# Linear attention joined to the block of the layers: o-products on two banks, rotation tables in its steps 5 to 8, local attention begun at its step 32

## The reference, cut to what matters

```python
# 1. gated linear attention, 2 heads of 64 (x is normalized and modulated before it)
q = silu(x @ Wq); v = x @ Wv; log_f = log_sigmoid(x @ Wk + delta); k = -expm1(log_f)
S = S * exp(g_t)[..., None] + k_t[..., None] * v_t[..., None, :]; o_t = q_t @ S      # over t
o = rms_norm_by_head(o * sigmoid(x @ G1 @ G2)) * norm_w; x = x + gate * (o @ Wo)
# 2. two layers on y = modulate(layernorm(x)):
#    local attention (8 heads of 64, windows of 64, rotary tables with scales), then a gated MLP
q = l2norm(q) * q_scale; k = l2norm(k) * k_scale; q, k = rotary_xpos(q, k)
y = y + local_attention(q, k, v) @ wo
y = y + (a * gelu(g)) @ w2 + b2                  # a, g = layernorm(shifted y) @ w1 + b1
# 3. a convolution-like attention   4. sixteen experts
```

## Time and profile before

| | us |
|---|---|
| median of 3 runs | 1184.93 (1182.98 to 1184.94) |
| profiled execution, its own time | 1182.32 |
| its span, first to last instruction | 1180.5 |
| PE busy | 1060.1 (90%) |
| DVE busy | 899.6 (76%) |
| ACT busy | 850.7 (72%) |
| POOL busy | 660.2 (56%) |

### The profile page before, as it was taken

One profiled execution on the slowest core, in us unless ns is written; L12 is line 12 of the kernel. 1 busy time (PEld: TensorE's weight loads), 2 busy tenths in 40 slices (PEclk: granted clock), 3 DMA queues, 4 the chain that ended last, 5 costly groups with the idle time before them and its releaser, 6 DMA issues. The chain is left out here.

```text
span 1180.5 us, 33825 instructions
## 1 busy us (share of the span) xinstructions
PE 1060.1 (90%) x11683; PEld 729.0 (62%) x11683; DVE 899.6 (76%) x2972; ACT 850.7 (72%) x2674; POOL 660.2 (56%) x1070
## 2 busy tenths in 40 slices
PE   6689996599999999789799999998899799999996
PEld 4466674267777776556477777776566488853442
DVE  4799998478888888565588888887475655289998
ACT  2678884488988898423589888987345766478886
POOL 1578985688888888200588888887133400002222
PEclk9899998799999999899899999999799999999999
DMA  7000000021321211131112222122000343200000
GB/s 237 3 2 10 11 3 1 16 49 38 71 54 47 50 45 47 39 120 34 40 38 47 47 47 47 38 47 47 21 1 20 85 112 86 49 6 17 17 19 18
DMA packets 66498, 50.86 MB, mean 43 GB/s; under 512 B 42262, under 2 KB 53442, under 8 KB 66050
## 3 DMA queue, kind: packets, MB, share of 16 engines
q1 hardware_dynamic: 66339, 48.84, 16.3%
HBM read 21.41 MB, written 2.38 MB: 20 GB/s over the span
## 5 line engine op out<-in xcount | busy, mean ns | idle before, releaser
L1168 PE MATMUL psum<-wa_wqkv,wa_hT 128*128 128x512 f32 x384 | 190.9, 606 | 4.4 <-DVE wa_tmp L1032 3.2
L1124 ACT ACTIVATE wa_p<-psum,wa_nb 128x128 f32<-128x128 f32 x512 | 184.2, 399 | 4.3 <-DVE wa_nb L1048 4.2
L1048 DVE CUSTOM_DVE_ANT_0 psum<-psum,wa_bias 128x128 f32<-128x128 f32 x512 | 133.0, 323 | 51.4 <-PE psum L1197 51.4
L1014 POOL TENSOR_TENSOR wa_p<-wa_p,wa_rrs 128x512 f32<-128x512 f32 x128 | 133.3, 1041 | 49.1 <-DVE wa_rrs L1057 49.1
L1709 POOL TENSOR_TENSOR ex_total<-ex_total,mod 128x128 f32<-128x128 f32 x32 | 15.5, 485 | 211.3 <-DVE ex_total L1837 211.3
L1124 ACT ACTIVATION_READ_ACCUMULATOR wa_p<-psum,wa_nb 128x1 f32 x512 | 122.7, 240 | 0.0
L1884 ACT ACTIVATE cv_z_ex_yw<-psum,ex_w 128x128 f32<-128x128 f32 x384 | 107.0, 401 | 20.1 <-DVE ex_w L1813 7.7
L1955 PE MATMUL psum<-ex_wc,ex_hT 128*128 128x512 f32 x256 | 117.9, 603 | 3.4 <-DVE cv_z_ex_yw L1820 2.1
L985 POOL TENSOR_TENSOR wa_qr<-wa_qr,wa_tmp 128x512 f32<-128x512 f32 x64 | 81.9, 1280 | 64.3 <-DVE wa_tmp L1032 64.3
L1134 ACT ACTIVATE wa_pT<-psum 128x512 f32<-128x512 f32 x128 | 76.6, 598 | 40.2 <-PE psum L1177 40.2
L1177 PE MATMUL psum<-ident,wa_p 128*128 128x128 f32 x512 | 81.4, 283 | 10.1 <-ACT wa_kT L1117 3.2
(11 more groups left out here) (258 smaller groups left out, 3007.2 us busy)
## 6 DMA issues: line engine op xcount, KB each, us to landing
wa_vm<-wa_v SPq DMA_DIRECT2D x127, 128.0 KB, 2.3
cv_toep<-cv_zpad SPq DMA_DIRECT2D x32, 136.0 KB, 2.7
cv_toep<-cv_zpad SPq DMA_DIRECT2D x16, 264.0 KB, 4.2
wa_tabs<-in_rotations_dram SPq DMA_DIRECT2D x2, 2048.0 KB, 8.0
wa_rows<-y_rows SPq DMA_DIRECT2D x31, 128.0 KB
wa_rows<-y_rows SPq DMA_DIRECT2D x31, 127.0 KB
x_rows<-in_L_attn_x_dram SPq DMA_DIRECT2D x4, 512.0 KB, 5.8
out_dram<-x_rows SPq DMA_DIRECT2D x32, 64.0 KB, 1.5
```

Source lines behind the costliest of these rows:

```text
L1014: nc.gpsimd.tensor_tensor(p, p, cols_bc(rrs[:, t % 2, r, :], P), ALU.mult)\
L1048: m = nc.vector.tensor_tensor_reduce(out=s, in0=s, in1=edges, scale=-1.0, scalar=MAX_FLOAT, op0=ALU.add, op1=ALU.min, accum_out=nb[:, t % ...
L1124: e = nc.scalar.activation(pr[:, t % 2, r, h, :], sim_bank[r][:, P * h:P * h + P], ACT.Exp, bias=nb[:, t % 2, r, h:h + 1], scale=-1.0, acc ...
L1168: nc.tensor.matmul(bank, hT[:, t % 3, :], wqkv[:, INNER * k:INNER * k + INNER], start=True, stop=True).then_inc(done.sem, 1)
```

## The change

1. `linear_attention` no longer has a block; it returns a `Phase` per engine, and its phase stands first in the timetable of the layers. `AttentionInputs.first_loads`, `stage` and so on are called as before; the first rows staged by attention's own SP list now wait for the y rows they need.
2. On ACT `values` moves from the head of a step with lag 2 to its end with lag 1, and on POOL all lags are one higher: within linear attention each engine's order stays the same, save at the few steps with additions between.
3. The tables are made one at a time before DVE's steps 5, 6, 7 and 8.
4. `o_project` of tile 29 and 31 writes to bank 6 (`out`), that of 30 to bank 7. Tile 29 waits for `gated` of tile 31, tiles 30 and 31 wait for the `residual` two tiles back.
5. Steps 0 to 7 of the first local attention come after the linear steps 32, 34, 36, 40, 41, 42, 43 and 44.
6. Attention and MLP take other banks (a plain renumbering 0, 1, 2, 3, 5, 6 to 2, 3, 5, 0, 6, 1, the same in both layers). Buffers of the layers now lie over those of linear attention, ordered so that the last needed are the last overwritten.
7. The ACT table load at the beginning of the first attention is gone; `wa_kT` is cleared before attention step 2, and of `ml_mT` only the last third, before attention step 10.

```diff
 class Phase:
-    def __init__(self, stages, first, n, between=None, begin=None):
+    def __init__(self, stages, first, n, between=None, begin=None, longer=None, more=0):
...
-def linear_attention(c, y, load_next, prepare_next):
+def linear_attention(c, y, given, ctx):
...
+    TWO_BANKS = TILES - 3
+    o_product = lambda t: out if t >= TWO_BANKS and (t - TWO_BANKS) % 2 == 0 else wide
...
-                unrolled([(keys, 0), (modulate, 13), (distances, 0)], 0, between={16: lambda: prepare_next.gpsimd(gp)})
+        return Phase([(keys, 1), (modulate, 14), (distances, 1)], 0, TILES, begin=begin,
+                     between={16: lambda: given.gpsimd(gp)})
...
-                between[36] = lambda: prepare_next.vector(dve)
+        for k in range(4):
+            between[5 + k] = lambda k=k: given.vector(dve, k)
...
-                unrolled([(values, 2), (decays, 3), (normalize, 0), (inverse_rms, 6), (exps, 1), (y_normalize, 14),
-                          (logs, 1), (h_columns, 0), (squares, 5), (sigmoids, 1), (end_keys, 2), (y_scale, 10)], 0,
+        return Phase([(decays, 3), (normalize, 0), (inverse_rms, 6), (exps, 1), (y_normalize, 14), (logs, 1),
+                      (h_columns, 0), (squares, 5), (sigmoids, 1), (end_keys, 2), (y_scale, 10), (values, 1)], 0, TILES,
...
-                    take("wide", v_res[1], t)
-                    nc.tensor.matmul(wide[:, 0:GH * E], ogT[:, t % 6, :],
+            if t == TWO_BANKS:
+                v_og.wait(pe, TILES - 1)
+            else:
+                v_res[1].wait(pe, t - 1 if t < TWO_BANKS else t - 2)
+            nc.tensor.matmul(o_product(t)[:, 0:GH * E], ogT[:, t % 6, :],
...
-    def vector(self, dve):
+    def vector(self, dve, k):
         self.wait_layer(dve, 0)
-        for k in range(4):
-            self.scale_table(dve, k)
+        self.scale_table(dve, k)
...
-    BANKS = ((0, 1, 2, 3, 4, 5, 6, 7), (0, 1, 2, 6, 7, 5, 4, 3))
+    BANKS = ((2, 3, 5, 0, 4, 6, 1, 7), (2, 3, 5, 1, 7, 6, 4, 0))
...
-                         begin=lambda: nc.scalar.preload_act_table_set("natural_log_exp_and_others"))
+                         begin=(lambda: nc.scalar.preload_act_table_set("natural_log_exp_and_others")) if l else None)
...
-        nc.gpsimd.memset(mT[...], 1.0)
+        nc.gpsimd.memset(mT[:, :, LAST, :], 1.0)
...
+    LINEAR, ATT, MLP = TILES + 14, TILES + 5, GROUPS + 4
+    MERGED = {32: 0, 34: 1, 36: 2, 40: 3, 41: 4, 42: 5, 43: 6, 44: 7}
...
+    for s in range(LINEAR):
+        timetable.append((0, s))
+        if s in MERGED:
+            timetable.append((1, MERGED[s]))
```

More of the change, by code:

```diff
@@ L175, in step @@
         for f, lag in self.stages:
-            if 0 <= s - lag < self.n:
+            if 0 <= s - lag < self.n + (self.more if f is self.longer else 0):
                 f(self.first + s - lag)
@@ L201, in linear_attention @@
     MAX_STEP, MAX_SIG_LOG = 20.0, 41.0
-    with ExitStack() as ctx:
-        sb = c.sb(ctx)
+    with ExitStack() as own:
+        sb = c.sb(own)
+        ring = lambda name, n, *shape: sb("la_" + name, [P, n, *shape])
+        eps, heads = sb("la_eps", [P, 1]), sb("la_heads", [P, GH])
+        yst, ymv = ring("yst", 2, 6), sb("la_ymv", [P, TILES, 2])
+        lyv, ys, yb = (sb("la_" + n, [P, TILES]) for n in ("lyv", "ys", "yb"))
+        lms, rr = ring("lms", 2, GROUP * GH), ring("rr", 2, GROUP * GH)
+        ogT, sq = ring("ogT", 6, P), ring("sq", 3, P)
+        wog = sb("la_wog", [P, B, GH, E])
+        qe, attn = ring("qe", 3, Q_SLOTS, P), ring("attn", 3, GH, P)
+        sg, vk = ring("sg", 4, 2, P), ring("vk", 4, 2, P)
+        state = [sb(f"la_state{b}", [P, P]) for b in range(B)]
+        masks = sb("la_masks", [P, NLEV, P], U32)
+        keep = sb("la_keep", [P, P])
+        dist, dec = ring("dist", 2, 1 + SLOTS * P), ring("dec", 2, SLOTS, P)
         cT, ex4, sig4, silu = (sb(n, [P, 4]) for n in ("cT", "c_exp", "c_sigmoid", "c_silu"))
@@ L226, in linear_attention @@
[L226 to L269, removed]
@@ new lines, in linear_attention, with in_turn @@
+    sem = lambda name: c.sem(ctx, "la_" + name)
+    signal = lambda name, every=1: Signal(sem(name), every=every)
+    def in_turn(name, n, every=1):
+        s = sem(name)
+        return [Signal(s, k, n, every) for k in range(n)]
+    c_in, w_in = sem("c_in"), sem("w_in")
+    x_in = [sem(f"x_in{k}") for k in range(TILES // CHUNK)]
+    g_set, v_set, a_set, p_set = sem("g_set"), sem("v_set"), sem("a_set"), sem("p_set")
+    v_xst, v_xb = in_turn("v_xst_xb", 2, CHUNK)
+    a_lx, a_xs = in_turn("a_log_xs", 2, CHUNK)
@@ L842, in first_loads, with stage_normalized @@
         self.load_layer(sp, 0)
+        self.y_done = y_done
         for i, n in self.PORTIONS[:self.AHEAD]:
-            y_done.wait(sp, i + n - 1)
-            self.stage(sp, "attention", 0, i, n)
+            self.stage_normalized(sp, i, n)
+    def stage_normalized(self, sp, i, n):
+        self.y_done.wait(sp, i + n - 1)
+        self.stage(sp, "attention", 0, i, n)
     def gpsimd(self, gp):
@@ L964, in sync @@
                 if not l and portion and 1 <= portion[0] <= len(PORTIONS) - AHEAD:
-                    given.stage(sp, "attention", l, *PORTIONS[portion[0] + AHEAD - 1])
+                    given.stage_normalized(sp, *PORTIONS[portion[0] + AHEAD - 1])
                 if i == 8:
@@ L1018, in gpsimd @@
             return Phase([(scale_q, 2), (scale_k, 2), (scale_p(0), 3), (add_q, 1), (clip, 1),
-                          (scale_p(1), 3), (add_k, 1)], first, TILES, begin=None if l else lambda: at_start(gp))
+                          (scale_p(1), 3), (add_k, 1)], first, TILES,
+                         between=None if l else {s: lambda f=f: f(gp) for s, f in between.items()})
         def vector(dve):
```

898 lines of the change are left out of this document (458 added, 440 removed).

## The result

| | before | after |
|---|---|---|
| median, us (20 runs each, side by side) | 1184.72 (1178.82 to 1190.11) | 1176.97 (1173.46 to 1185.00) |
| ratio of the runs | | 0.9934, 95% interval 0.9920 to 0.9948 |
| span of the profiled execution, us | 1180.5 | 1172.2 |
| PE busy | 1060.1 (90%) | 1062.9 (91%) |
| DVE busy | 899.6 (76%) | 897.0 (77%) |

Faster by 0.66%, 7.8 us. The forecast of 1176.5 us was met to half a microsecond. The profile shows that this is luck in good part: the seam gained 3.6 us less than forecast, the tables cost 2.3 us less, what was forecast behind the seam cost less too, and the errors cancel.

What follows compares the result with a forecast made beforehand. Seam bound by waits and list order, attention behind it by PE, linear attention mostly by DVE. -11.9 + 0.8 + 0.3 + 3.3 = -7.5 us gave 1174.8; median placed 1.7 above, 1176.5 us, range 1173 to 1180.

Steps and rivals of the forecast that it cites:

- The sum: Whole kernel: seam -11.9, POOL's modulation 0.8, memset 0.3 and tables 3.3 give -7.5 us, 1174.8 us; median placed at 1176.5.
- Tables: Linear steps 5 to 8: each table lengthens its step by 0.8 us to 5.4, 3.3 us in all, bounds 2.0 to 5.1.
- Seam: From linear attention to the layers: first attention scores start 11.9 us earlier, at 216.6 us; bounds 9.8 to 14.4.
- The delay by ACT: Linear step 33: attention step 0 holds ACT at h_columns, so the decays of tile 30 start 1.5 us late.
- the clock term: Seam: low clock between linear step 35 and attention step 3 only, costing 1.5 plus 1.0 us, 2.5 in all.
- The queue behind step 1: Seam: linear step 35, with base_level and PE's last output, queues behind attention step 1; 6.6 and 3.1 us in series.
- Behind the scores: After the first scores: POOL's modulation in linear steps 41 to 45 costs 0.8 us, the mT memset 0.3.
- The signs named: Changed profile: scores near 220 us, table steps 5.4, residuals 1.3, decays 1.5 late, clock low only before scores, constant shift.
- Rival 1: Seam: no real overlap, inserted steps only stand in line; 9.8 us won there, total -5.4, 1178.5 to 1180 us; chance 0.17.
- Rival 2: Seam and tables: full overlap at 2.4 GHz, -14.4 + 2.0 = -12.4 us, 1170 to 1172 us; chance 0.12.
- Rival 3: Merged stretch: small pieces keep PE's clock low through attention steps 3 to 5, some 6 us a step, 1187 us; chance 0.04.
- Rival 4: Linear attention: regular steps take 0.2 us longer in all 30, eating 6 us; within 2 us of before; chance 0.05.

Runs made afterwards that it cites:

- 5: The changed kernel with every output product in bank 7 instead of two banks; ratio to the kernel before 0.9962, scores 40.8 us from tile 29.
- 9: The changed kernel with attention step 0 kept behind linear step 32, steps 1 to 7 moved behind 36 and 40 to 45; ratio to before 0.9894, scores 38.3 us from tile 29.
- experiment 4: The changed kernel with attention step 0 moved from linear step 32 to 34, right ahead of step 1; ratio to before 0.9894, scores 35.9 us from tile 29.
- 6: The changed kernel with attention steps 0 and 1 both behind linear step 35; ratio to before 0.9917, scores 33.8 us from tile 29.
- 1: The kernel before with only the rotation tables moved to DVE's linear steps 5 to 8; ratio to before 0.9949, tile 20 at 223.7 us from tile 29.
- 2: The kernel before with only the last output products on two banks; ratio to before 0.9973, scores 47.3 us from tile 29.
- 3: The changed kernel with no attention step among the linear ones; block, tables and banks stay; ratio to before 0.9878, scores 37.3 us from tile 29.
- 10: The changed kernel with attention steps 0 to 7 behind linear steps 36, 38 and 40 to 45; ratio to before 0.9877, scores 32.6 us from tile 29.
- 7: The changed kernel with attention steps 0 to 5 behind linear steps 36 and 40 to 44; ratio to before 0.9874, scores 34.3 us from tile 29.

## Why the prediction was right, step by step

**The sum.** Forecast -11.9 + 0.8 + 0.3 + 3.3 = -7.5 us. Measured at attention's tile 0: -8.3 for the seam, 1.0 for the tables, 0 for POOL and the memset: -7.3 (its residual at 246.39 against 253.66). At the end of the span it is 8.3, and 7.8 between the medians. The sum is right by luck, since none of its terms is: the seam brought 3.6 us less, the tables cost 2.3 us less, and of the 1.1 us for POOL and the memset nothing had come by tile 0 and 0.3 later on. The step from the profiled execution to the median has its share too: I placed the median 1.7 us above the sum, and it lies 3.0 above the profiled execution, 1176.97 to 1173.95, while the sum of 1174.8 was 0.9 too high.

**Tables, mis-sized: 3.3 us, measured 1.0.** I took 5.4 us for the length of a step; it was 4.96 to 5.00. (Four times 0.8 is 3.2; the 3.3 is a slip of 0.1.) The starts of DVE's instructions tell why. From `base_level` to clip it took 63.80 - 63.11 = 0.69 us before and 60.52 - 60.19 = 0.33 after: that is the wait for PE's projection, marked as 0.24. From `scaled` to the running sum 1.31 became 1.19, the wait for the log. These two I had, as 0.24 and 0.10. But the distances to `query` (1.28 to 1.13), to `keep_levels` (0.35 to 0.20) and to `base_level` (0.46 to 0.33) shrank as well, by waits too short to be marked in a row. Together 0.91 us, so that a table whose successor starts 1.19 us after it lengthens the step by 0.28. Over all: from `scaled` to `scaled` the four steps were 4.31, 4.55, 4.68 and 4.68 us and are 4.97, 5.00, 4.96 and 5.00, in sum 1.7 us more, and the next two won 0.7 back. 1.0 is under my lower bound of 2.0. That bound let a table of 1.28 us fill all the time in which DVE is not busy, 0.79 us, but 0.91 us were there to fill and the table takes up only 1.19 of a step. And "so it is not won back" was wrong by those 0.7 us. That I added nothing for the contention with POOL was right: POOL is busy 4.52 us of a step with a table, 3.51 before, and no row of DVE there waits for it.

**Seam, mis-sized: 11.9 us, measured 8.3.** By its own terms, after, from DVE's step 33 at 184.09:

| part | forecast at full clock | measured |
|---|---|---|
| attention step 0, linear steps 33 and 34 | 1.5 + 7.45 = 8.95 | 11.23 (to 195.32) |
| attention step 1 | 6.6 | 8.15 (to 203.47) |
| linear steps 35 and 36 | 3.1 + 1.3 = 4.4 | 5.09 (to 208.56) |
| attention step 2 | 5.9 | 7.57 (to 216.13) |
| steps 37 to 40, to the scores | 5.2 | 5.13 (to 221.26) |
| sum | 31.05 + 2.5 for the clock = 33.55 | 37.17 |

The delay by ACT was sized right: `scaled` comes 186.49 - 184.09 = 2.40 us into the step and came 0.95 us into it before, 1.45 more for the 1.5. The residuals too: 216.65 to 217.92 is 1.27 us, for 1.3. What failed is the place and size of the clock term, 2.5 us. I had it fall "between linear step 35 and attention step 3 only". It fell at 188.7 us already, at the end of linear step 33, where I had called the steps "as before", so that linear step 34 and much of what follows ran at 1.2 GHz as well, and the whole is 6.1 us over the terms at full clock instead of 2.5 (how much of the 6.1 is the clock's was not taken apart). That it is attention step 0's place that brings this is shown by its removal: in the three kernels that have step 0 behind linear step 32 (after, 5 and 9) the clock falls within linear steps 33 and 34, in the nine that have not it stays at 1.00 there, each by one profile. Moving it is worth 4.4 us (experiment 4), three times the 1.5 us of the wait. That PE's idle time of 1.2 us before the scores of step 33 is what drops the clock fits the rows but was not tried by itself.

**The queue behind step 1, in the sum but not seen as a choice.** The prediction has linear step 35, "and so PE's last output", queued behind attention step 1, and adds the two in series. That is how it runs, and another place is cheaper: 2.1 us from 4 to 6 (35.9 and 33.8), 2.0 us from the change to 9 (40.3 and 38.3), though in 6 step 0 moves too, and in 9 all later steps. That the 2.0 us are PE's wait for `base_level` alone is not shown.

**Behind the scores, mis-sized: 1.1 us forecast, 0.3 measured.** From the first scores to tile 0's residual it is 25.13 us after and 25.17 before; both hold one step at a low clock, and in 1, 2, 3, 9 and 10, which have none, it is 23.7 to 23.8. The change could have won these 1.4 us as well. POOL's y rows stand right before `scale_q`, in its timeline after,

```profile
220.49 0.46 POOL L326 TENSOR_TENSOR y_rows<-y_rows,mod 128x128 f32<-128x128 f32 x1
221.02 0.45 POOL L328 TENSOR_TENSOR y_rows<-y_rows,mod 128x128 f32<-128x128 f32 x1
221.43 1.04 POOL L1017 TENSOR_TENSOR wa_qr<-wa_qr,wa_rn 128x512 f32<-128x512 f32 x1
```

and cost little: PE's steps there are 7.95, 8.01, 7.88 and 8.01 us, against 7.89 before. From tile 0 to tile 8 the residuals are 0.3 us further apart than before, in two steps of 8.02 and 8.01 us and one of 7.95, the only one that experiment 3 has too. The step after the first scores is 9.18 us, over the 8.5 that I had named as a sign of error; in the row 221.26:230.44 the clock is at 0.73, and before a step of the same stretch took 9.29 us.

**The signs named.** Held: scores near 220 (221.26), single table rows, residuals at 1.3, decays 1.5 us late, steps of linear attention from 10 on equal within 0.05 us. Did not hold: table steps of 5.4 us, the clock's place, the constant shift. The shift is 7.0 to 7.3 us through the first layer's attention, then between 6.0 and 11.9 us, 8.3 at the end; the later seams differ by as much among kernels that are alike there.

**The rivals.** Rival 1, that each inserted step only stands in line, is the nearest account of the seam: with no step inserted at all (experiment 3) it is 3.0 us shorter at the scores than with three. Its figure of -9.8 for the seam is 1.5 us from the measured -8.3, mine 3.6. Its total of 5.4 us came out too small because it shared my terms for the tables and POOL. What it lacked is that inserting can cost more than nothing. Rival 2 (full overlap, -14.4) is what experiments 6, 7 and 10 reach in size, with 14.8, 14.3 and 16.0 us, by placing the steps behind the recurrence; its full clock they have not, since in all three the clock is at 1.2 GHz for a while before the scores. Rival 3, the clock kept low by pieces, was right in kind and too large: the clock is at 1.2 GHz in three spells, from 188.7, 202.4 and 219.4 us, each of them over in 7 to 10 us. The Trainium skill, TensorE: Matmul & The Clock Gate, HAM oscillation, warned of this; in this trace the clock does go down, up and down again, 0.71, 0.50, 0.80, 0.73, 1.00 by stretch, and the change is faster all the same. Rival 4 did not happen.

## What to carry to other kernels

Where two chains are laid into one in-order list, ask at each insertion what of the old chain is queued right behind it and who waits for that: here the first scores come 5.7 us later with attention's first step inside the recurrence (9) than with it behind (10; its second step stands elsewhere too). An insertion's price is its wait and what comes with it, here a fall of the clock; together they were three times the wait alone. Measure each part of a change by itself: here the tables' move alone came within 0.4 us of the whole to tile 20, and one part, the interleaving, took 3.0 us away. And when filler work is put into a step that is bound by a loop of short waits, expect it to fill waits too short to be marked: read the distances between the starts of the instructions, and not the marked idle time alone, and look whether the steps that follow win some of it back.

## What was not expected of the hardware

The clock of TensorE at the start of linear attention differs from execution to execution of nearly the same instructions: in steps 5 to 8 it was 1.00 in some kernels' profiles and 0.50 for one to nearly all of them in others, which places tile 29 anywhere from 180.83 to 184.52 us among the kernels with the early tables. The two kernels without them were profiled at 179.77 and 179.90; whether the tables make the low clock likelier stays open. It is likely one reason why the 20 runs of the changed kernel reach over 11.5 us, more than its whole gain, and why the comparison needed positions and not only totals.
